# Inverted-residual convolution: patches turned in 32x32 blocks by VectorE, projection in 4 row by 2 column tiles, depthwise column tiles on the two halves of the image

## The reference

```python
# x: (4, 48, 128, 128).  First layer (not touched by the change): 8x8-window attention with
# layer norm, then layer norm, a 48 -> 192 -> 48 MLP with gelu, both with residuals.
# Second layer, the convolution block:
h = jnp.einsum('oc,bchw->bohw', w1, x)                  # expand, 48 -> 288 channels
h = jax.nn.relu(_bn(h, g1, b1, m1, v1))
h = jax.lax.conv_general_dilated(h, wd, (1, 1), ((1, 1), (1, 1)), feature_group_count=HID)
h = jax.nn.relu(_bn(h, gd, bd, md, vd))                 # depthwise 3x3
h = jnp.einsum('oc,bchw->bohw', w2, h)                  # project, 288 -> 48 channels
return x + _bn(h, g2, b2, m2, v2)
```

## Time and profile before

| | |
|---|---|
| median of 3 runs | 1954.3 us (1952.6 to 1955.3) |
| profiled execution: span | 1952.0 us |
| median less the span | 2.3 us |
| PE busy, share of the span | 1870.2 us, 96% |
| DVE (VectorE) busy | 1445.8 us, 74% |
| ACT (ScalarE) busy | 1322.8 us, 68% |
| POOL (GpSimd) busy | 647.1 us, 33% |
| granted TensorE clock, mean | 0.993 |
| HBM read and written | 94 GB/s over the span |

### The profile page before, as it was taken

The page is one execution under the profiler, slowest core; times in us unless marked ns, Lnnn a source line. Parts: engine busy times, 40 slices in busy tenths (PEclk is TensorE's granted clock), DMA queues, the critical chain, the costliest instruction groups (busy, mean ns, idle before and its releaser), DMA issues.

```text
span 1952.0 us, 74705 instructions
## 1 busy us (share of the span) xinstructions
PE 1870.2 (96%) x29960; PEld 1565.2 (80%) x29960; DVE 1445.8 (74%) x2650; ACT 1322.8 (68%) x2838; POOL 647.1 (33%) x869
## 2 busy tenths in 40 slices
PE   5999999999999996999999999999999999999998
PEld 4888888888888885555555899999999999999997
DVE  5999999999999997666667556566566566566564
ACT  2788878878888885555555666666666666666665
POOL 4333333333333333413100434325334343344240
PEclk9999999999999998999999999999999999999999
DMA  2222222222222222777664444545363454445331
GB/s 67 68 73 76 78 73 76 77 73 76 77 72 77 74 76 77 182 171 179 161 150 111 97 108 126 99 113 126 87 147 86 112 137 102 103 129 105 99 111 34
DMA packets 286410, 198.43 MB, mean 102 GB/s; under 512 B 225991, under 2 KB 275672, under 8 KB 276504
## 3 DMA queue, kind: packets, MB, share of 16 engines
q1 hardware_dynamic: 282114, 189.12, 37.9%
q0 software_dynamic: 2368, 6.25, 1.5%
q10 hardware_dynamic: 1750, 0.39, 0.1%
HBM read 128.36 MB, written 54.72 MB: 94 GB/s over the span
## 4 chain that ended last, share of the span: by engine, by line
PE 56%; ACT 2%; DMA 1%; issue 1%; DVE 0%; SPq 0%; ACTq 0%; DVEq 0%
PE psum L1126 14%; PE psum L1145 13%; PE psum L1171 9%; PE psum L1180 5%; PE psum L680 5%; PE psum L661 3%; PE psum L651 3%; PE psum L666 2%; ACT h2T L1227 1%; DMA room<-tok_mid 1%; ACT h L884 1%; DMA room<-in_ident 0%; ACT room L750 0%; DVE room L885 0%; DVE room L712 0%
## 5 line engine op out<-in xcount | busy, mean ns | idle before, releaser
L934 POOL TENSOR_TENSOR mats<-mats,dscale 112x2048 f32<-112x2048 f32 x72 | 260.8, 3622 | 315.0 <-DMA mats<-in_taps 312.6
L1126 PE MATMUL psum<-ew,xp 64*100 64x96 f32 x6144 | 322.4, 252 | 16.8 <-ACT h L884 13.5
L885 DVE TENSOR_SCALAR h<-psum 100x384 f32<-100x384 f32 x384 | 211.9, 557 | 151.7 <-PE psum L1126 141.6
L1126 PEld LDWEIGHTS psum<-ew,xp 64*100 64x100 f32 x6144 | 295.5, 165 | 26.3 <-ACT h L884 18.6
L1227 ACT ACTIVATE h2T<-psum 96x1024 f32<-96x1024 f32 x192 | 195.6, 1019 | 177.5 <-PE psum L1180 177.5
L1145 PE MATMUL psum<-h,mats 101*64 101x128 f32 x4608 | 269.2, 274 | 1.6 <-issue 0.9
L1145 PEld LDWEIGHTS psum<-h,mats 101*64 101x64 f32 x4608 | 252.0, 137 | 11.8 <-issue 2.0
L884 ACT ACTIVATE room<-psum 64x512 f32<-64x512 f32 (+1 forms) x384 | 206.1, 537 | 78.1 <-PE psum L1145 71.5
L344 PE MATMUL psum<-kb,qa 128*64 128x256 f32 x2048 | 244.0, 380 | 0.8 <-DVE prob L443 0.8
L885 DVE TENSOR_SCALAR room<-psum 64x512 f32<-64x512 f32 (+1 forms) x288 | 174.2, 605 | 64.7 <-PE psum L1145 58.8
L884 ACT ACTIVATE h<-psum 100x384 f32<-100x384 f32 x384 | 186.6, 486 | 48.1 <-PE psum L1126 34.1
(11 more groups left out here) (154 smaller groups left out, 3228.3 us busy)
## 6 DMA issues: line engine op xcount, KB each, us to landing
mats<-in_taps SPq DMA_DIRECT2D x69, 896.0 KB, 5.9
tok_mid<-mid SPq DMA_DIRECT2D x128, 224.0 KB, 1.9
room<-tok_mid SPq DMA_DIRECT2D x64, 448.0 KB, 4.4
piece<-img_mid SPq DMA_DIRECT2D x196, 63.8 KB, 2.4
img_mid<-room SPq DMA_DIRECT2D x128, 97.5 KB, 3.0
kb<-kk SPq DMA_DIRECT2D x512, 24.0 KB
out<-yc SPq DMA_DIRECT2D x32, 384.0 KB, 4.5
scratch<-in_x_tokens SPq DMA_DIRECT2D x126, 96.0 KB, 1.9
```

The costliest lines, as they stand in the source:

```text
L885: return nc.vector.tensor_scalar(dst, src, 0.0, None, ALU.max)
L934: nc.gpsimd.tensor_tensor(m, m, bc(scale[0:MROWS, at:at + TCH], 2, POUT), ALU.mult).then_inc(mats_scaled, 1)
L1126: mm = nc.tensor.matmul(ring[(j + u) % 4][0:PIN, p:4 * CH:4], xp[hx][rows, 2 * j + p, :], w1[rows, c, :], start=True, stop=True)
```

## The change

The order of pixels in `mats` changes (in `placed_taps`), so that 32 of a patch's 64 pixels are its left 4 columns and 32 its right 4. In depthwise, the two column tiles now hold the matrix of the same channel, and take the left and the right 64 patches as moving operand; a unit's results lie in two full banks (units 4 and 5 use the four banks of `ps_y`), and each is emptied by one instruction of 128 partitions, 9 of 12 by ScalarE and 3 by VectorE. The expand order of patches is changed, and ScalarE empties the right bank too for the first three pairs. The PE transposes, their two PSUM banks and ScalarE's copy are gone; `h2T` takes the free half of `room`, and VectorE transposes `h2` in 32x32 blocks, 32 channels and half of the patches in one instruction. `w2` is laid four times, in groups of 32 partitions. A chunk has 4 projection steps; a step multiplies 3 blocks of 32 channels (accumulated) in 4 groups of 32 rows by 2 column tiles, 256 columns each, and has 4 additions of 256 elements. The store of `y` is one piece per half, and by rows in the last.

```diff
+BLK = 32
+CBLKS = CH // BLK
+GROUPS4 = P // BLK
-EXPANDS = PATCHES // 4
+PAIRS_E = PATCHES // 8
+DPARTS = 2
...
-        w2 = sb("pw", [P, CHUNKS, NT])
+        w2 = sb("pw", [P, CHUNKS, CBLKS, NT])
...
+        h2T = room[:, PATCHES // 2 * CH:PATCHES * CH].rearrange("q (e p x) -> q e p x", e=CBLKS, x=BLK)
-        h2T = [sb(f"h2T{s}", [P, 2, PART * POUT]) for s in range(2)]
-        ps_t = psum[:, 4:6, :]
-        ps_y = [psum[:, 6 + s, :] for s in range(2)]
+        ps_y = psum[:, 4:8, 0:PATCHES // 2 * BLK // 8]
-        NSTEP = len(STEPS)
+        NSTEP = PC // 2
+        SEGMENTS = (7, 3, 3, 3)
+        ACT_ALONE = (0, 1, 2)
+        DVE_FILTERED = (1, 3, 5)
+        BANK_OF = (0, 2, 0, 2, 4, 6)
+
+        def expand_by_act(J, u):
+            return u == 0 or J in ACT_ALONE
+
+        def filter_by_act(d, part):
+            return part == 0 or d not in DVE_FILTERED
...
+        def evacuate_filter(by_act, d, part):
+            ch = DUNIT * d + DUNIT // DPARTS * part
+            dst = h2[:, :, ch:ch + DUNIT // DPARTS].rearrange("q p (b n) -> q p b n", n=4)
+            src = psum[:, BANK_OF[d] + part, :].rearrange("q (b p n) -> q p b n", b=2, n=4)
             return relu(by_act, dst, src)
...
+            def store(h):
+                sp.wait_ge(y_done, NSTEP * CHUNKS * (h + 1) + 1)
...
+            def bank_free(k, J, u):
+                if J >= 2:
+                    pe.wait_ge(*expands_done(k, J - 2, u))
+                elif k and u == 0:
+                    pe.wait_ge(unit_act, act_filtered(k - 1, 2 + J))
+                    pe.wait_ge(unit_dve, dve_filtered(k - 1, 2 + J))
...
                 if d == 0:
-                    emptied(k, 0)
-                if d >= 2:
-                    emptied(k, d - 1)
+                    pe.wait_ge(unit_act, act_expanded(k))
+                    pe.wait_ge(unit_dve, dve_expanded(k))
+                elif d in (2, 3):
+                    pe.wait_ge(unit_act, act_filtered(k, d - 2))
+                    wait(pe, unit_dve, dve_filtered(k, d - 2))
+                elif d == 4:
+                    pe.wait_ge(y_done, NSTEP * k + 1)
+                for n in range(DUNIT):
+                    ch = DUNIT * d + n
+                    at = 4 * (PATCHES // 2) * (n % 8 // 4) + n % 4
                     for u in range(2):
-                        ch = DUNIT * d + DUNIT // 2 * u + n
-                        bank = psum[POUT * u:POUT * u + POUT, 4 * (d % 2) + u + 2 * (n // 4), :]
-                        mm = nc.tensor.matmul(bank[:, n % 4:4 * PATCHES:4], mats[ch // TCH][0:PIN + 1, ch % TCH, :],
-                                              h1[0:PIN + 1, ch, :],
+                        mm = nc.tensor.matmul(psum[POUT * u:POUT * u + POUT, BANK_OF[d] + n // 8, at:at + 4 * (PATCHES // 2) - n % 4:4],
+                                              mats[ch // TCH][0:PIN + 1, ch % TCH, :],
+                                              h1[0:PIN + 1, ch, PATCHES // 2 * u:PATCHES // 2 * (u + 1)],
                                               start=True, stop=True)
...
                 def project(n):
+                    pe.wait_ge(turned, TURNS * k + TURNS - 1 + (n >= NSTEP // 2))
+                    if n or last:
+                        pe.wait_ge(y_done, NSTEP * k + n + 1)
...
+                    for e in range(CBLKS):
+                        for g in range(GROUPS4):
+                            for r in range(2):
+                                lanes = slice(BLK * g, BLK * g + BLK)
+                                mm = nc.tensor.matmul(ps_y[64 * r:64 * r + 64, g, :], w2[lanes, c, e, :],
+                                                      projected(lanes, e, r, n, last), start=(e == 0), stop=(e == CBLKS - 1))
-                def turn(n):
-                            mm = nc.tensor.transpose(turned_at(n, last)[0:CH, r, POUT * p:POUT * p + POUT],
-                                                     h2[rows, PR * pc + a + p, :], ident[rows, rows])
...
+                for n in range(NSTEP):
+                    if not last:
+                        for J in pairs_at(n):
+                            expand(k + 1, (c + 1) % CHUNKS, (hx + 1) % 2 if c == CHUNKS - 1 else hx, J)
+                    project(n)
+                if not last:
+                    depthwise(k + 1, 0)
...
-                    nc.scalar.activation(h2T[n % 2][0:CH, :, :],
-                                         turned_at(n, last)[0:CH, :, 0:POUT * PART], ACT.Copy).then_inc(copied, 1)
...
+            def turn(k, e, half, last):
+                dve.wait_ge(unit_act, act_filtered(k, 2 * e + 1))
+                dve.wait_ge(unit_dve, dve_filtered(k, 2 * e + 1))
+                nc.vector.transpose(turned_patches(h2T[:, e, :, :], half, last),
+                                    turned_patches(h2[:, :, BLK * e:BLK * (e + 1)], half, last)).then_inc(turned, 1)
...
             def chunk(b, hx, c, last):                                  # VectorE
+                filtered(k, 1)
+                filtered(k, 2)
+                for half in range(2):
+                    turn(k, 0, half, last)
+                filtered(k, 3)
+                filtered(k, 4)
+                for half in range(2):
+                    turn(k, 1, half, last)
+                filtered(k, 5)
+                for half in range(2):
+                    turn(k, 2, half, last)
...
+                    for i, J in enumerate(pairs_at(n)):
+                        if n and i < 2:
+                            for g in (2 * i, 2 * i + 1):
+                                add(n - 1, g, b, hx, c, k, last)
+                        expanded(k + 1, J)
+                if not last:
+                    for g in range(GROUPS4):
+                        add(NSTEP - 1, g, b, hx, c, k, last)
+                    filtered(k + 1, 0)
...
-                placed[:, (r + t // 3) * (PW + 2) + c + t % 3, :, r * PW + c] = taps[:, :, t]
+                placed[:, (r + t // 3) * (PW + 2) + c + t % 3, :, c // 4 * BLK + r * 4 + c % 4] = taps[:, :, t]
```

More of the change, by code:

```diff
@@ L861, in conv @@
[L861 to L865, removed]
-        def ready_before_depthwise(k):
-            return ready_before_expand(k) + EXPANDS
-        def act_before_expand(k):
-            return (EXPANDS // 2 + ACT_OUT[DEPTHS]) * k
-        def dve_before_expand(k):
-            return (EXPANDS // 2 + DVE_OUT[DEPTHS]) * k
@@ new lines, in conv, with expands_done @@
+        BANK_OF = (0, 2, 0, 2, 4, 6)
[3 more added lines that the diff above has]
+            return part == 0 or d not in DVE_FILTERED
+        def expands_done(k, J, u):
+            if expand_by_act(J, u):
+                return unit_act, (E_ACT + F_ACT) * k + sum(expand_by_act(i, v) for i in range(J) for v in range(2)) + u + 1
+            return unit_dve, (E_DVE + F_DVE) * k + sum(not expand_by_act(i, 1) for i in range(J + 1))
@@ new lines, in act_expanded, with dve_expanded, act_filtered, dve_filtered @@
+        def act_expanded(k):
+            return (E_ACT + F_ACT) * k + E_ACT
+        def dve_expanded(k):
+            return (E_DVE + F_DVE) * k + E_DVE
+        def act_filtered(k, d):
+            return act_expanded(k) + sum(filter_by_act(i, part) for i in range(d + 1) for part in range(DPARTS))
+        def dve_filtered(k, d):
+            return dve_expanded(k) + sum(not filter_by_act(i, part) for i in range(d + 1) for part in range(DPARTS))
+        def ready_expand(k, J, u):
+            return READY * k + 2 * J + u + 1
@@ L943, in _ @@
         def _(pool):
[L945 removed]
+            constants = [(t[...], 0.0) for t in (w1, w2, *c2.values(), *piece)]
             constants += [(eps[:, :], EPS)]
@@ L1123, in expand @@
                         rows = slice(ONE * u, ONE * u + ONE)
-                        if p == 3 and u == 0:
-                            wait(pe, copied, copies)
-                        mm = nc.tensor.matmul(ring[(j + u) % 4][0:PIN, p:4 * CH:4], xp[hx][rows, 2 * j + p, :],
+                        mm = nc.tensor.matmul(ring[(2 * J + u) % 4][0:PIN, p:4 * CH:4], xp[hx][rows, 4 * J + p, :],
                                               w1[rows, c, :], start=True, stop=True)
@@ L1154, in first @@
                 pe.wait_ge(border_set, 2)
-                for j in range(0, EXPANDS, 2):
-                    expand(0, 0, 0, j)
+                for J in range(PAIRS_E):
+                    expand(0, 0, 0, J)
                 depthwise(0, 0)
@@ L1271, in chunk @@
             def chunk(b, hx, c, last):
                 k = number(b, hx, c)
-                filtered(k)
-                for n in range(NSTEP + 1):
-                    if not last:
-                        expanded(k + 1, units_at(n))
-                    for m in projected_at(n):
-                        add(m, b, hx, c, k)
+                filtered(k, 1)
[3 more added lines that the diff above has]
+                filtered(k, 3)
@@ L1280, in first @@
+                if not last:
+                    for g in range(GROUPS4):
```

(6 more changed lines are left out.)

268 lines of the change are left out of this document (119 added, 149 removed).

## The result

The changed kernel takes **1928.2 us** (median of 4 runs, 1921.9 to 1930.9), the kernel before 1953.9 beside it: ratio 0.987, 95% interval 0.985 to 0.989. It is faster, by 26 us (1.3%) and not by 176; 1778 was forecast and 1860 was the upper end of the range. The profiled execution took 1929.1 us, its span 1927.3, so 1.8 are outside the span (the prediction took 2.3, a median less the span of another execution).

A forecast was written before the change was run, and what follows sets the result against it. TensorE was taken to bound `conv`, with VectorE level after the change: 23 periods falling from 36.1 to 28.5 us give 174.8, the last chunk and first unit 1.9; 1952.0 less these, plus 2.3 outside the span, is 1778 us, range 1733 to 1860.

The forecast's parts named there:

- Depthwise keeps 192 records: TensorE's depthwise per chunk: 192 records of 64 columns at 29.7 ns, 5.7 us against 11.0, saving 5.3.
- no gain in depthwise: Rival, depthwise: one column tile's load doesn't run beside the other's matmul; period 31.9 us, 1858 in all; 5%.
- I take 0 for both: Closer tap loads with the thinner border margin, and one store per half, were each taken to cost 0 us.
- The rival on transfers: Pieces, borders or the store come 5 us later than allowed at each of 7 changes of half: 35 us, 1813; 12%.
- The clock: TensorE's granted clock, 1.00 in the old profile; a value under 1.00 was named as a sign of being wrong.
- Transposes: VectorE's six transposes of 128x1024 a chunk, each taken at 1.22 us from line 443.
- the rivals on half rate and on the rate of line 113: VectorE transposes at 2.44 us, 1953 in all, 4%; or at 0.65 us like line 113, 1733 in all, 8%.
- Projection, eight tiles abreast: TensorE's projection: eight tiles run together, 1.6 us a step, 6.4 a chunk, saving 1.2.
- ScalarE 14.5, VectorE 23.5 a chunk: Work per chunk: ScalarE 14.5 us, from 23.7; VectorE 23.5, or 24.7 with 0.03 allowed between instructions.
- Segments 4.3: Three times a chunk, three expand pairs, waits and a projection step on TensorE: 4.3 us each.
- Pair 5 waits 1.8 for VectorE: In expand, pair 5 needs pair 3's bank, which VectorE empties behind the transposes: TensorE waits 1.8 us.
- Borders: Setting the next half's last border before its first expand: margin falls to 1.8 us, no wait expected.

The follow-up runs named there:

- half_and_small: Changed kernel with half_depthwise and small_both together: every second depthwise channel left out from chunk 1 on, tap loads and seven stores cut; 1752.8 us.
- small_both: Changed kernel with each tap load bringing 8 of 112 rows and the stores of all halves but the last writing 4 of 128 rows; 1850.7 us.
- small_store: Changed kernel with the stores of all halves but the last writing 4 of 128 rows; 1877.1 us.
- small_loads: Changed kernel with each tap load bringing 8 of its 112 rows, 64 KB instead of 896 KB; 1888.9 us.
- half_depthwise: Changed kernel computing only every second depthwise channel from chunk 1 on, 192 records a chunk in place of 384; 1857.9 us.
- loads_paced: Changed kernel with each later tap load issued only after the one before landed, and the first behind a store only after the store landed; 1937.4 us.
- store_in_eight: Changed kernel with a half's store issued at the same place as eight transfers of 192 KB instead of two of 768 KB; 1900.8 us.
- loads_in_quarters: Changed kernel with each half's store as four pairs, each behind its projection step, and each tap load issued as four of 224 KB; 1870.6 us.
- old_depthwise: Changed kernel with the depthwise back in its earlier form, 192 records of 128 columns and 24 evacuations a chunk; 1906.5 us.

## Why the prediction was wrong

Three terms give the whole distance from the forecast to the result, each between two kernels that were run:

| term | by | us |
|---|---|---|
| forecast | | 1778 |
| the rest of the sum was too dear | half_and_small 1752.8 | -25 |
| 384 short records, not 192 | small_both 1850.7 less 1752.8 | +98 |
| transfers that starve TensorE | result 1928.2 less 1850.7 | +77 |

- **"Depthwise keeps 192 records"** failed, and it is a miscount, not a property of the chip. The group has 160 records for 80 channels of 128 columns, two a channel. In the diff the loop over `u`, which took two channels abreast, now goes over the two halves of one channel, so each channel has two matmuls of 64 columns: 384 records. The price of a record (29.7 ns, taken from the earlier trace rows) was right: 29.8 measured; 384 x 29.7 = 11.4 against 11.0 is no gain, where the sum had -5.3. The rival "no gain in depthwise" had this part of the outcome, 1858 at a period of 31.9, by another cause, so that it came near is luck: small_both shows 1850.7 at 31.6. A check of columns would have caught it: the same columns at the same rate for a pair of tiles can't take half the time.
- **"I take 0 for both"** (SyncE and the store) failed. The rival on transfers had looked for late data and priced it at 7 x 5 us. After the change no data is late; what comes late is TensorE's own instructions, and the clock falls at 11 of the 23 stops. Neither was in the sum. It cost 77 us; cutting the store alone gives 51 back (small_store), the loads alone 39 (small_loads), so the two overlap.
- **The clock** was taken as 1.00. It was 0.974 over the span, and the prediction's own sentence on what would show it wrong, a granted clock under 1.00, is what the profile has.
- **Transposes** 1.22: measured 1.224. Right, and the rivals on half rate and on the rate of line 113 fall.
- **Projection, eight tiles abreast**, 1.6 a step: measured 1.49. Nearly right.
- **Additions** 0.418, and 0.06 more with the scalar: 0.418, 0.428 with the image added, 0.478 with the scalar. Right.
- **ScalarE 14.5, VectorE 23.5 a chunk**: measured 14.1 and 21.9. The single instructions were priced right (they add up to 23.3), but back to back they overlap by 0.08 us, two transposes in 2.37 and four additions in 1.42, where the prediction added 0.03 between them. The period is 27.4 on the forecast's own terms, not 28.5: pair 5 waits 0.6 less, and three segments are 0.2 shorter each.
- **Segments 4.3**: measured 4.09.
- **Pair 5 waits 1.8 for VectorE**: it does not wait at all in the changed kernel, since the longer depthwise gives VectorE time; on the forecast's own terms 1.17.
- **Borders**: no wait after the change. The thin margin that the prediction saw was real: five waits in half_depthwise, four in loads_paced.

What stays open: whether it is the size of a packet or of a transfer that decides how long an instruction packet waits, since store_in_eight and loads_in_quarters changed both together, and with them how far apart the bytes are issued. Nor is the split of the 77 us into stops and lower clock measured.

## What to carry to other kernels

Count the records of a new loop from its own indices and check them against the columns, before multiplying by a rate. A tile form that turns long matmuls into twice as many short ones also doubles the rate at which TensorE uses up its instructions, and near big transfers that is paid twice, in stops and in the clock behind them: look at the instruction queue beside the chain wherever a stop has the releaser "issue". Here a q8 packet ended 1.2 to 1.7 us before TensorE resumed from a starved stop; the 24 waits of old_depthwise with the same releaser showed no such order, and were for ScalarE. Then spread large transfers over the work and cut them into smaller ones; in this kernel that alone was worth 58 us, more than twice what the change brought.

## What the runs showed of the hardware that I had not expected

- TensorE's instructions come in packets of 16 KB over the same 16 DMA engines, one for 128 records (a load and a matmul each) in this code. At 29.7 ns a record that is one every 3.8 us.
- Behind two stores of 768 KB no such packet came for 10 us: around the stop at 1616.22 one ended at 1610.5, and the next started at 1620.53.
- At 11 of 23 stops, of 1.3 to 7.3 us, the granted clock fell to its lower level, for 3.4 to 10.2 us each; the ten longest stops are among them.
- The recorded times of VectorE's instructions overlap by 0.08 us where they stand back to back: four additions of 0.418 take 1.42.
- 48 records of 32x64 tiles with 256 columns, four row tiles by two column tiles, take 1.48 us.
